# The zero-point correction of the down projection moved into the accumulation, with f32 tiles up to the transpose

## The reference

```python
xn = layernorm(x)
q, k, v = rope(xn @ Wq.T), rope(xn @ Wk.T), xn @ Wv.T      # 16 heads of 128
# scores are taken between the heads of one token, not between tokens
attn = softmax(q @ k.T / sqrt(128)) @ v
a = attn @ Wo.T
gate = silu(xn @ ((wq_gate - 128) * s_gate).T)             # 8-bit weights, scale per row
up = xn @ ((wq_up - 128) * s_up).T
f = (gate * up) @ ((wq_down - 128) * s_down).T             # 5632 -> 2048
return x + a + f
```

## Time and profile before

| | before |
|---|---|
| median of 2 runs | 3111.19 us (3110.34 to 3112.03) |
| the profiled execution's own time | 3110.08 us |
| its span, slowest core (core 5) | 3108.5 us |
| spans of the 8 cores | 3100.9 to 3108.5 us |
| mean granted TensorE clock | 0.967 to 0.970 |
| TensorE busy | 2958.4 us (95%) |
| VectorE / ScalarE / GpSimd busy | 459.1 / 489.7 / 159.6 us |

### The profile page before, as it was taken

One profiled execution on the slowest core, in us unless ns is written; L12 is line 12 of the kernel. 1 busy time (PEld: TensorE's weight loads), 2 busy tenths in 40 slices (PEclk: granted clock), 3 DMA queues, 4 the chain that ended last, 5 costly groups with the idle time before them and its releaser, 6 DMA issues.

```text
span 3108.5 us, 34323 instructions; the slowest of 8 cores (3100.9 to 3108.5 us)
## 1 busy us (share of the span) xinstructions
PE 2958.4 (95%) x14327; PEld 1379.5 (44%) x14327; DVE 459.1 (15%) x1021; ACT 489.7 (16%) x749; POOL 159.6 (5%) x306
## 2 busy tenths in 40 slices
PE   4999999999999999999949999999999999999997
PEld 2444464444444434444424444544444444444443
DVE  3001071000000011111131001700000000111111
ACT  4000072121212100000040000721212121000000
POOL 0000000000000001000000000000000000011010
PEclk9999969999999999999969999799999999999999
DMA  5222201212212144464461222011212212444744
GB/s 137 82 77 73 82 15 55 82 68 82 77 73 82 68 158 150 153 228 152 170 153 68 82 76 74 15 65 71 82 70 80 82 68 87 156 152 145 247 145 153
DMA packets 50071, 321.12 MB, mean 103 GB/s; under 512 B 5817, under 2 KB 5872, under 8 KB 22272
## 3 DMA queue, kind: packets, MB, share of 16 engines
q0 software_dynamic: 42816, 268.59, 24.2%
q1 hardware_dynamic: 4672, 33.56, 3.7%
q10 hardware_dynamic: 2432, 16.78, 2.0%
HBM read 209.85 MB, written 16.78 MB: 73 GB/s over the span
## 4 chain that ended last, share of the span: by engine, by line
PE 91%; ACT 3%; DMA 2%; DVE 2%; issue 1%; ACTq 0%; DVEq 0%; POOL 0%; POOLq 0%; SPq 0%
PE p L601 39%; PE p L428 21%; PE p L715 19%; PE p L699 7%; PE p L395 1%; ACT xn_b L333 1%; DMA xbuf<-x 1%; PE pb L470 1%; DMA dwst<-wd 1%; DVE rs L555 1%; PE p L521 0%; DMA wst<-wo 0%; PE pb L528 0%; PE pb L666 0%; PE p L490 0%
## 5 line engine op out<-in xcount | busy, mean ns | idle before, releaser
L601 PE MATMUL p<-xnT,wst 128*128 128x512 bf16 x5632 | 1219.9, 380 | 0.0
L601 PEld LDWEIGHTS p<-xnT,wst 128*128 128x128 bf16 x5632 | 552.1, 98 | 667.0 <-issue 5.2
L428 PE MATMUL p<-xnT,wst 128*128 128x512 bf16 x3072 | 665.4, 380 | 0.0
L715 PE MATMUL p<-actT,dwst 128*128 128x512 bf16 x2816 | 621.7, 380 | 8.1 <-DMA dwst<-wd 8.1
L428 PEld LDWEIGHTS p<-xnT,wst 128*128 128x128 bf16 x3072 | 301.1, 98 | 363.5 <-issue 2.7
L715 PEld LDWEIGHTS p<-actT,dwst 128*128 128x128 bf16 x2816 | 276.0, 98 | 343.9 <-issue 14.4
L621 DVE TENSOR_TENSOR actT<-gate_b,up_b 128x512 bf16<-128x512 bf16 x176 | 74.8, 425 | 1151.0 <-ACT up_b L616 1151.0
L699 PE MATMUL p<-attnT,wst 128*128 128x512 bf16 x1024 | 238.3, 387 | 2.4 <-DMA wst<-wo 2.4
L610 ACT ACTIVATE gate_b<-p,sgT 128x512 bf16<-128x512 f32 x176 | 120.9, 687 | 490.8 <-PE p L601 490.8
L616 ACT ACTIVATE up_b<-p,suT 128x512 bf16<-128x512 f32 x176 | 120.9, 687 | 474.7 <-PE p L601 474.7
L699 PEld LDWEIGHTS p<-attnT,wst 128*128 128x128 bf16 x1024 | 99.2, 99 | 116.0 <-issue 13.3
(11 more groups left out here) (71 smaller groups left out, 843.3 us busy)
## 6 DMA issues: line engine op xcount, KB each, us to landing
wst<-wgu POOLq DMA_DIRECT2D x88, 1024.0 KB, 5.2
dwst<-wd POOLq DMA_DIRECT2D x128, 704.0 KB, 4.2
wst<-wo POOLq DMA_DIRECT2D x32, 1024.0 KB, 7.2
wst<-wq POOLq DMA_DIRECT2D x16, 1024.0 KB, 5.8
wst<-wk POOLq DMA_DIRECT2D x16, 1024.0 KB, 5.4
wst<-wv POOLq DMA_DIRECT2D x16, 1024.0 KB, 5.6
out_nat<-x SPq DMA_DIRECT2D x4, 4096.0 KB, 18.9
y<-out_nat SPq DMA_DIRECT2D x8, 1024.0 KB, 9.5
```

The lines of the kernel that those rows point to most:

```text
L428: e.matmul(o, s, r, start=stt, stop=sp),
L601: e.matmul(o, s, r, start=stt, stop=sp),
L715: e.matmul(o, s, r, start=stt, stop=sp),
```

## The change

The L642 matmuls, their copies L645 and the two `corr` buffers go. In their place each block's down accumulation gets a 45th matmul, `cneg` by `hilo_ac`, into the same bank, so that the bank holds h @ wq_down.T - 128 * sum(h) when it is read. The first of the two outT operations (`t_cp`) is then a plain copy of `wobank`, and runs on ScalarE. `outT0` and `outT1` become f32, and with them the transposes (identity `eye_f` in place of `eye_b`), their PSUM tiles (the same banks, seen as f32: 512 elements fill a bank) and what L673 reads. The semaphore of the second operation waits for the 45th matmul. Nothing else changes: neither the streams of weights, nor the order of blocks and tails.

```diff
--- before.py
+++ after.py
@@ -135,8 +135,8 @@
     up_b = at("up_b", [128, 1024], BF16, A0 + 2048)
     dwst0 = at("dwst0", [128, 2816], BF16, A0)
     dwst1 = at("dwst1", [128, 2816], BF16, A0 + 5632)
-    outT0 = at("outT0", [128, 512], BF16, A0 + 11264)
-    outT1 = at("outT1", [128, 512], BF16, A0 + 13312)
+    outT0 = at("outT0", [128, 512], F32, A0 + 11264)
+    outT1 = at("outT1", [128, 512], F32, A0 + 13312)
     wst0 = at("wst0", [128, 4096], BF16, 180224)
     wst1 = at("wst1", [128, 4096], BF16, 188416)
     m = 196608
@@ -169,7 +169,6 @@
     hilo_ac = hilo_xn
     lo_b = ata("lo_b", [1, 512], BF16, 1024)
     scl_stage = ata("scl_stage", [44, 384], F32, 1536)
-    corr_sb = [ata("corr0", [128, 512], F32, 2048), ata("corr1", [128, 512], F32, 2048)]
     assert BASE + m <= 229376 - 512, f"sbuf over budget: {BASE + m}"
 
     p0 = nc.alloc_psum_tensor("p0", [128, 512], F32)
@@ -182,8 +181,6 @@
     pb7 = nc.alloc_psum_tensor("pb7", [128, 1024], BF16)
     pf4 = pb4[:].bitcast(F32)
     pf5 = pb5[:].bitcast(F32)
-    pf6 = pb6[:].bitcast(F32)
-    pf7 = pb7[:].bitcast(F32)
     PBF = [p0, p1, p2, p3]
     ALLP = [p0, p1, p2, p3, pb4, pb5, pb6, pb7]
 
@@ -216,7 +213,6 @@
         "xnT_free": None,
         "ln_xbuf_done": None,
         "outT_free": [None, None],
-        "corr_free": [None, None],
     }
 
     P.add("gpsimd", lambda e: e.dma_start(eye_f[:], deye), inc="dsc", amt=16)
@@ -633,19 +629,6 @@
                        war=mx(st_["actT_read"] if c > 0 else None))
         last_wo = None
         last_dn = None
-        corr_toks = [None, None]
-        for tb in range(2):
-            pcb = [pb6, pb7][tb]
-            pcf = [pf6, pf7][tb]
-            t_cm = P.add("tensor",
-                         lambda e, o=pcf[0:128, 0:512], s=cneg[:], r=hilo_ac[:, tb * 512:(tb + 1) * 512]:
-                         e.matmul(o, s, r, start=True, stop=True),
-                         waits=mx(hilo2, tok_cneg, bank_free[id(pcb)]), inc="ST")
-            t_ce = P.add("scalar",
-                         lambda e, o=corr_sb[tb][:], s=pcf[0:128, 0:512]: e.activation(o, s, AF.Copy),
-                         waits=mx(t_cm, st_["corr_free"][tb]), inc="SS")
-            bank_free[id(pcb)] = t_ce
-            corr_toks[tb] = t_ce
         for tb in range(2):
             rows = c * CH + tb * 512
             dnv = out_nat[:].rearrange("p (j cc) -> p j cc", j=4)
@@ -663,12 +646,12 @@
                     t_tr = P.add("tensor",
                                  lambda e, o=tp[:, j * 128:(j + 1) * 128],
                                         s=ot[:, j * 128:(j + 1) * 128]:
-                                 e.transpose(o, s, eye_b[:]),
+                                 e.transpose(o, s, eye_f[:]),
                                  waits=mx(t_st, bank_free[id(pbank)]) if j == 0 else [],
                                  inc="ST" if j == 3 else None)
                 st_["outT_free"][oc % 2] = t_tr
                 dnv3 = out_nat[:].rearrange("p (j cc) -> p j cc", j=4)[:, :, oc * 128:(oc + 1) * 128]
-                pv3 = tp[:, 0:512].rearrange("p (j cc) -> p j cc", j=4)
+                pv3 = tp.rearrange("p (j cc) -> p j cc", j=4)
                 t_ad = P.add("vector",
                              lambda e, o=dnv3, s0=pv3, s1=dnv3: e.tensor_tensor(o, s0, s1, ALU.add),
                              waits=mx(t_tr, t_pre, prev_add[0]), inc="SV")
@@ -703,7 +686,6 @@
                     wslot_free[wo_sl] = t_mm
                 wt = mx(d_tok0, bank_free[id(dbank)], act_done)
                 wt22 = mx(d_tok1)
-                t_dmm = None
                 for hc in range(HCN):
                     piece_sl = d_sl0 if hc < 22 else d_sl1
                     cbase = (hc % 22) * 128
@@ -711,34 +693,33 @@
                     t_dmm = P.add("tensor",
                                   lambda e, o=dbank[:], s=DWST[piece_sl][:, cbase:cbase + 128],
                                          r=actT[:, hc * 1024 + tb * 512: hc * 1024 + tb * 512 + 512],
-                                         stt=(hc == 0), sp=(hc == HCN - 1):
-                                  e.matmul(o, s, r, start=stt, stop=sp),
+                                         stt=(hc == 0):
+                                  e.matmul(o, s, r, start=stt, stop=False),
                                   waits=(wt if hc == 0 else (wt22 if hc == 22 else [])), inc=inc)
                     if hc == 21:
                         dslot_free[d_sl0] = t_dmm
                     if hc == HCN - 1:
                         dslot_free[d_sl1] = t_dmm
-                last_dn = t_dmm
+                t_dn = P.add("tensor",
+                             lambda e, o=dbank[:], s=cneg[:], r=hilo_ac[:, tb * 512:(tb + 1) * 512]:
+                             e.matmul(o, s, r, start=False, stop=True),
+                             waits=mx(hilo2, tok_cneg), inc="ST")
+                last_dn = t_dn
                 ot = outT0 if oc % 2 == 0 else outT1
-                t_cp = P.add("vector",
-                             lambda e, o=ot[:], s0=corr_sb[tb][:], sc=sdT[:, oc:oc + 1],
-                                    s1=wobank[:]:
-                             e.scalar_tensor_tensor(o, s0, sc, s1, ALU.mult, ALU.add),
-                             waits=mx(t_mm, corr_toks[tb], tok_sd,
-                                      st_["outT_free"][oc % 2], st_["ln_xbuf_done"],
-                                      st_["attn_scr_free"]), inc="SV")
+                t_cp = P.add("scalar", lambda e, o=ot[:], s=wobank[:]: e.activation(o, s, AF.Copy),
+                             waits=mx(t_mm, st_["outT_free"][oc % 2], st_["ln_xbuf_done"],
+                                      st_["attn_scr_free"]), inc="SS")
                 bank_free[id(wobank)] = t_cp
                 t_st = P.add("vector",
                              lambda e, o=ot[:], s0=dbank[:], sc=sdT[:, oc:oc + 1], s1=ot[:]:
                              e.scalar_tensor_tensor(o, s0, sc, s1, ALU.mult, ALU.add),
-                             waits=mx(t_dmm, t_cp, tok_sd), inc="SV")
+                             waits=mx(t_dn, t_cp, tok_sd), inc="SV")
                 bank_free[id(dbank)] = t_st
                 if pend[0] is not None:
                     do_tail2(*pend[0])
-                pend[0] = (ot, pb4 if oc % 2 == 0 else pb5,
+                pend[0] = (ot, pf4 if oc % 2 == 0 else pf5,
                            pb4 if oc % 2 == 0 else pb5, t_st, oc)
             do_tail2(*pend[0])
-            st_["corr_free"][tb] = t_cp
             wst_toks = mx(*add_toks)
             for j in range(4):
                 P.add("sync" if j % 2 == 0 else "scalar",
```

## The result

| | before | after |
|---|---|---|
| median | 3111.2 us | 3144.6 us |
| ratio of the times, 95% interval | | 1.0108 (1.0095 to 1.0121) |
| the profiled execution's own time, its span | 3110.1, 3108.5 us | 3141.7, 3139.9 us |
| one steady step of the out phase | 13.18 us | 13.86 us |
| the two out phases together, mean over the cores | 917.6 us | 950.3 us |

The change costs 33.4 us, 1.1%. The forecast was 13.9 us, so the sign and the class (within 2%) are right and the size is not: 3144.6 lies inside the range, but 2.4 times what was forecast was lost.

What follows compares the result with a forecast made beforehand. TensorE, busy 95% of the span, was taken as the bound, with no hole in the steady out-phase step. Terms 13.8 + 12.3 - 5.3 - 5.2 - 1.7 = +13.9 us on 3111.2 gave 3125 us, range 3111 to 3152.

Steps and rivals of the forecast that it cites:

- the class (within 2%): Whole kernel: time changes by no more than 2% either way, chance 0.95; slower by more 0.04, faster by more 0.01.
- The cneg matmul: Out phase, 64 times: takes its neighbours' spacing of 0.216 us, its two-row weight load hidden; +13.8 us.
- The f32 transposes: Out-phase tails: 107 ns each at full clock, load hidden, 51 ns extra on 240 transposes; +12.3 us.
- the four passes: Skill's rule for true f32, applied to the tails: 224 ns per transpose, +40 us; not the one adopted.
- the transpose mode: Skill's mode, four times faster for f32, applied to the tails: the part would cost about nothing; not the one adopted.
- The start and its clock: Start of both out phases: first L699 earlier, -5.3 us; first stretches at full clock, -5.2 us.
- The stalls on weight pieces: L715's four waits for dwst, 8.1 us: each shortens by 0.42 us of longer cover; -1.7 us.
- ScalarE's copy: Out phase: 64 copies of about 0.6 us on an engine without work there; 0 us, no TensorE wait.
- The rivals: Mostly f32 transpose prices: free 0.10, load exposed 0.20, four bf16 costs 0.12, over 2% 0.03; clock low at start 0.03.
- the prediction's own sign: Steady out-phase step: 13.6 us as forecast; 13.4 free, 13.9 load exposed, 14.0 four costs, over 14.4 slower by over 2%.
- the f32 weight load is not hidden: Rival on the out-phase transposes: their load shows, +29.0 us, 3140 us, step 13.9 us; chance 0.20.

Runs made afterwards that it cites:

- e1: The changed kernel with cneg and the rounded sums stored on 128 rows, the added moving rows zero; ratio to before 1.0058, +18.0 us.
- e3: The kernel before with f32 outT, transposes and banks alone; ratio to before 1.0042, +13.1 us.
- e6: The kernel before with each chunk's two L642 matmuls and their copies moved behind block 0's down matmuls; ratio to before 0.9973, -8.4 us.
- e2: The changed kernel with outT, the transposes and their banks in bf16 again, cneg still on 2 rows; ratio to before 1.0055, +17.1 us.
- e8: The changed kernel with cneg and the sums on 64 rows, 62 of them zeros; one execution, 3142.6 us.
- e4: The changed kernel with cneg on 128 rows and bf16 outT and transposes; ratio to before 1.0026, +8.1 us.

## Why the prediction was wrong

**The cneg matmul: the step that failed.** The prediction had "its two-row weight load of 94 ns fits under the 216, so it takes their spacing". A load of 94 ns would fit, but it isn't placed there. 64 matmuls cost 13.8 us of spacing, as said, and 0.10 + 0.10 + 0.06 us more each (two exposed loads, and the gap inside the f32 transposes that goes with them): 16 us by the spacings, 15.6 by e1. The forecast had nothing for these. That is all but 4 us of the miss. The trace of before held it. In the attention phase L521 is a 9-row matmul between full ones, and in a stretch at full clock its timeline reads:

```profile
1970.79 0.39 PE L516 MATMUL p<-Kb,Qb 128*128 128x128 bf16 x4
1971.11 0.39 PE L521 MATMUL p<-mkB,mkA 9*128 9x512 bf16 x1
1971.43 0.40 PE L528 MATMUL pb<-eye_b,Vb 128*128 128x128 bf16 x4
```

The last of the four L516 starts 3 x 0.056 after 1970.79, at 1970.96, so L521 comes 0.15 us behind a matmul of 128 columns that takes 0.056, and L528 0.32 us behind one of 512 that takes 0.216. Both 0.1 us are there. I looked instead at the two L642 and divided 0.92 us by two, though the clock changed over them (granted 0.56 from 1111.5 to 1112.5, 0.50 behind). In the second chunk the second L642 starts at 2659.64 and the first L699 at 2660.20, 0.56 us later at granted clock 0.50, where L699s come every 0.43: the exposed load could be seen there too.
The Trainium skill, TensorE: Matmul & The Clock Gate, section Step-by-step: what each phase is for, says that a weight load is pulled ahead of running matmuls when row groups don't conflict or when it goes to the background weight buffer. For loads of equal rows the traces agree (0.21 us ahead in e1). That a change in the number of rows ends it is shown by the runs only, for 2, 9 and 64 rows.

**The f32 transposes: right.** 107 ns forecast, 109 measured, the load hidden. The reading of the two scale transposes at half clock gave the right price, with some luck: the earlier trace rows shows that they differ in rows too (44 and 16) and not in columns alone, as the prediction says. The Trainium skill gave two rules beside it, by estimates from them 224 ns for the four passes (FP8 and Floating Point Precision, section TensorE Precision Notes) and 56 ns for the transpose mode (TensorE: Matmul & The Clock Gate, section Terms); e3 measures a spacing between the two, a factor of two from either. e3 gives +13.1 us, against 12.3.

**The start and its clock: right.** 10.5 us forecast, 9.8 measured in the traces of all cores, and e6 turns them into 8.4 us of time.

**The stalls on weight pieces: no gain.** I forecast -1.7 us because the cover of each piece grows by 0.42 us. The waits did fall in the second halves, from 5.0 to 3.2 and from 5.8 to 5.5 us, but the cold start of before had also been cover: it put the second block's first piece behind the reload. Taking 5 us away there made a new wait of 2.2 us (mean over the cores) with low clock behind it, and the whole is +0.3. With the starts and the waits as measured in the traces and the rest by the spacings the sum closes: 13.8 + 16 + 12.3 - 9.8 + 0.3 = 32.6 us, against 32.7 in the out phases. What the low clock behind the waits costs, before and after, is not measured by itself.

**ScalarE's copy: right.** 64 copies of 0.60 us; the only wait of TensorE that names one is the row of 0.8 us told above.

**The rivals.** None was the case, and the prediction's own sign would have misled: it gave 13.9 us per step and 3140 us to "the f32 weight load is not hidden", and 13.86 us and 3144.6 were measured. A reader of the step or the time alone would have taken that for the cause. The exposed loads were those around the cneg matmul, which no rival had; the spacings inside the step and e3, with f32 transposes alone at 13.39 us, told them apart.

## What to carry to other kernels

Price an added matmul by its spacing in a place where its neighbours have another shape, not by its recorded length or its load's. Here a narrow contraction (2, 9 or 64 rows between neighbours of 128) cost its columns and two exposed weight loads, and padding it with zero rows removed both. When a stall at a phase's start is taken out, ask which transfer it had let finish, and look at the next block's wait. A gate on progress does nothing if what it gates is held up longer by something else.

## What the runs showed of the hardware

- A bf16 matmul of 512 columns with 2, 9 or 64 rows between matmuls of 128 rows starts 0.10 us late and delays the next by 0.10 us (after, e2, e8 and L521 of before; spacings 0.31 and 0.32 in place of 0.216); with 128 rows there is no delay (e1, e4).
- In front of f32 transposes such a matmul costs 0.06 us more inside their group: four take 0.50 us behind 2 rows and 0.44 behind 128 (after, e1); with bf16 transposes it is 0.23 and 0.22 (e2, e4).
- An f32 transpose of 128 x 128 takes 109 ns in a stream at full clock, 1.95 times a bf16 one (56 ns); its load, recorded at 140 ns, is hidden (e3).
- Taking out two waits of 3.5 us for a small copy, of which 1.8 us each remain as a wait for VectorE, and the half clock that followed them shortened the starts of the two out phases by 9.8 us together (after, e6).
